# Low parts of the FFN's activations on GpSimd, bias of the output product on VectorE, in a schedule of its own

## What is computed

```
xn = layernorm(x)
q, k, v = xn @ wq + bq, xn @ wk + bk, xn @ wv + bv      # 16 heads of 16, rotary embedding on q and k
a  = softmax(causal(q k^T / 4)) v
s  = a @ wo + bo
h  = silu(xn @ w_gate^T) * (xn @ w_up^T)                # hidden width 768, int8-range weights / 127
g  = silu(h @ w_down^T)
out = x + s * g
```

## Time and profile before

| | us |
|---|---|
| median of 3 runs (lowest, highest) | 553.73 (550.44, 556.63) |
| profiled execution: whole time | 555.2 |
| profiled execution: span of the profile | 553.7 |
| TensorE busy in it | 480.0 (87%) |
| VectorE busy | 425.1 (77%) |
| GpSimd busy | 332.1 (60%) |
| ScalarE busy | 330.0 (60%) |

### The profile page before, as it was taken

One profiled execution on the slowest core, in us unless ns is written; L12 is line 12 of the kernel. 1 busy time (PEld: TensorE's weight loads), 2 busy tenths in 40 slices (PEclk: granted clock), 3 DMA queues, 4 the chain that ended last, 5 costly groups with the idle time before them and its releaser, 6 DMA issues.

```text
span 553.7 us, 13804 instructions
## 1 busy us (share of the span) xinstructions
PE 480.0 (87%) x5397; PEld 367.7 (66%) x5397; DVE 425.1 (77%) x667; ACT 330.0 (60%) x683; POOL 332.1 (60%) x439
## 2 busy tenths in 40 slices
PE   0679899979989999998999988999999988889873
PEld 0466797857667766785778675777668666558633
DVE  3398879946898799978996798769987768875713
ACT  2663256645785666666666756655674756663670
POOL 2114087745687938876779658598747646425452
PEclk9989799997999999999999999999989989977988
DMA  9356214394436856645753833578535575862021
GB/s 290 110 178 167 83 53 135 114 213 128 105 75 212 197 160 181 158 130 148 170 140 95 223 85 88 160 176 216 136 93 134 164 174 155 158 151 64 3 78 38
DMA packets 59667, 76.65 MB, mean 138 GB/s; under 512 B 15056, under 2 KB 30928, under 8 KB 59600
## 3 DMA queue, kind: packets, MB, share of 16 engines
q1 hardware_dynamic: 58512, 74.68, 51.4%
q10 hardware_dynamic: 1088, 1.05, 0.6%
HBM read 41.91 MB, written 29.82 MB: 130 GB/s over the span
## 4 chain that ended last, share of the span: by engine, by line
PE 38%; DVE 25%; DMA 13%; ACT 8%; issue 7%; SPq 6%; POOL 2%; DVEq 0%; ACTq 0%; POOLq 0%
PE ps_w L618 22%; DVE row_max L982 9%; PE ps_w L749 5%; DMA sum_rows<-o_t 5%; PE ps_w L647 4%; ACT probs L863 4%; PE ps_w L663 4%; DMA at_lo<-inv_rows 4%; DVE h_lo L434 3%; DVE hid L1028 2%; DVE hid L1023 2%; DVE attn L991 2%; PE ps_w L650 2%; DVE high_low L972 1%; SPq L549 1%
## 5 line engine op out<-in xcount | busy, mean ns | idle before, releaser
L982 DVE TENSOR_REDUCE row_max<-ps_w 128x2 f32<-128x1024 f32 (+3 forms) x256 | 199.7, 815 | 42.0 <-PE ps_w L650 41.6
L863 ACT ACTIVATE probs<-ps_w 128x512 f32<-128x512 f32 (+1 forms) x384 | 181.0, 535 | 78.1 <-PE ps_w L663 65.2
L1094 POOL TENSOR_SCALAR_AFFINE_SELECT probs<-probs 128x256 f32<-128x256 f32 x256 | 109.4, 449 | 123.1 <-ACT probs L863 122.9
L647 PE MATMUL ps_w<-k_st,q_st 48*128 48x512 f32 (+3 forms) x512 | 80.8, 355 | 19.5 <-DVE row_max L982 6.5
L663 PE MATMUL ps_w<-q_st,k_st 49*128 49x512 f32 (+3 forms) x512 | 78.8, 353 | 16.0 <-DMA q_st<-minus_max 5.8
L618 PE MATMUL ps_w<-xt_hi,wgu_hi 64*128 64x512 f32 x384 | 84.9, 430 | 3.0 <-DVE wgu_lo L961 1.3
L618 PE MATMUL ps_w<-xt_lo,wgu_hi 64*128 64x512 f32 x384 | 80.4, 407 | 0.0
L749 PE MATMUL ps_w<-probs,vals 128*32 128x512 f32 (+3 forms) x1024 | 79.1, 450 | 0.7 <-POOL probs L1094 0.4
L647 PEld LDWEIGHTS ps_w<-k_st,q_st 48*128 48x128 f32 x512 | 49.1, 195 | 39.8 <-issue 11.8
L663 PEld LDWEIGHTS ps_w<-q_st,k_st 49*128 49x128 f32 x512 | 47.2, 193 | 35.0 <-ACT probs L863 8.7
L749 PEld LDWEIGHTS ps_w<-probs,vals 128*32 128x32 f32 x1024 | 29.1, 112 | 41.0 <-issue 29.7
(11 more groups left out here) (106 smaller groups left out, 904.3 us busy)
## 6 DMA issues: line engine op xcount, KB each, us to landing
parts_q<-high_low SPq DMA_DIRECT2D x48, 256.0 KB, 3.2
q_st<-parts_q SPq DMA_DIRECT2D x64, 192.0 KB, 3.6
k_st<-parts_k SPq DMA_DIRECT2D x64, 192.0 KB, 4.7
parts_k<-high_low SPq DMA_DIRECT2D x42, 256.0 KB, 3.4
xn<-L_attn_x SPq DMA_DIRECT2D x8, 512.0 KB, 4.0
res<-L_attn_x SPq DMA_DIRECT2D x8, 512.0 KB, 6.2
result<-res SPq DMA_DIRECT2D x8, 512.0 KB, 3.6
attn<-o_t SPq DMA_DIRECT2D x112, 32.0 KB, 2.6
```

Of the source, the lines that this page charges most:

```text
L647: pe.matmul(dst[h][:, col:col + (t + 1) * P], q_st[64 * h:64 * h + STACK, pair, t * P:(t + 1) * P], k_st[64 * h:64 * h + STACK, pair, 0:(t ...
L863: nc.scalar.activation(probs[:, (pair % 2) * SLOTS + slot, col:col + WIDTH[c]], w_of(kind, b, 3 * pair + c // 2, c % 2)[:, 0:WIDTH[c]], AC ...
L982: last = nc.vector.tensor_reduce(of_pair, both_of(kind, b, i)[:, :, col:col + (t + 1) * P], AX.X, ALU.max)
L1094: nc.gpsimd.affine_select(out=v, in_=v, compare_op=ALU.is_ge, fill=0.0, base=0, pattern=[[0, 2], [1, P]], channel_multiplier=-1).then_inc( ...
```

## The change

`POOL_LOWS` becomes all six tiles, so that the subtraction of `low_part` runs on GpSimd for each of the 48 hidden tiles. The items `GB` (GpSimd) and `BO` (ScalarE) and their semaphores go. In `OP`, VectorE first adds `bo_row`, unscaled, to the product in PSUM, in place, and then does the multiplication it did. The rest of the program text is as it was, but the table of orders is another on all five engines.

```diff
-POOL_LOWS = ()
+POOL_LOWS = (0, 1, 2, 3, 4, 5)
...
     "pool": """
-        WC0.0 WQ0.0 RS0.0 RP3.0 RP4.0 RS0.1 NM0.1 NM1.1 NM2.1 NM3.1 RP0.1 RP1.1 RP3.1 RP4.1 RS0.2 B0.0 NM0.2 RP6.1 NM1.2 B1.0 NM2.2 NM3.2
+        WQ0.0 RS0.0 RP3.0 RP4.0 RS0.1 WC0.0 HL0.0 HL1.0 NM0.1 NM1.1 NM2.1 NM3.1 HL2.0 HL3.0 HL4.0 RP0.1 RP1.1 HL5.0 RP3.1 B0.0 RP4.1 RS0.2
...
         def add_x(eng, tensor_tensor, b, i):
             need(eng, prod_ready, 2 * b + i + 1)
-            need(eng, bias_added, 2 * b + i + 1)
+            if i == 0:
+                need(eng, res_in, 16 * (b + 1))
...
-                elif kind == "BO":
-                    act.wait_ge(bias_in, 16 * 4)
-                    nc.scalar.activation(bo_row[:], bo_row[:], ACT.Identity, scale=0.5 * WSCALE).then_inc(bo_scaled, 1)
...
                 elif kind == "OP":
                     wait_full(dve, "dve", kind, b, 0, i)
                     ps = w_of(kind, b, 0, i)
-                    need(dve, bias_added, 2 * b + i + 1)
+                    by_tile = lambda ap: ap.rearrange("p (a d) -> p a d", d=DM)
+                    if b == 0 and i == 0:
+                        dve.wait_ge(bias_in, 16 * 4)
+                    nc.vector.tensor_tensor(by_tile(ps[:, :]), by_tile(ps[:, :]), by_tile(bo_row[:]).broadcast_to([P, 2, DM]), ALU.add)\
+                        .then_inc(sum_ready, 1)
+                    need(dve, sum_ready, 2 * b + i + 1)
                     nc.vector.scalar_tensor_tensor(out=gate[:, b % 2, i, :], in0=ps[:, :], scalar=0.5 * WSCALE, in1=gate[:, b % 2, i, :],
                                                    op0=ALU.mult, op1=ALU.mult).then_inc(prod_ready, 1)
...
-                elif kind == "GB":
...
-                    need(pool, silu_ready, 2 * b + i + 1)
-                    need(pool, *rope_t_used[-1])
-                    need(pool, bias_added, 2 * b + i)
...
-                    nc.gpsimd.tensor_tensor(by_tile(rope_t[:]), by_tile(gate[:, b % 2, i, :]), by_tile(bo_row[:]).broadcast_to([P, 2, DM]), ALU.mult)\
-                        .then_inc(gate_biased, 1)
...
-                    nc.gpsimd.tensor_tensor(r, r, rope_t[:], ALU.add).then_inc(bias_added, 1)
```

More of the change, by code:

```diff
@@ new lines @@
+        B23.1@45 U1.3 A9.2@23 PV3.1@4 A10.2@01 B0.2@57 V0.3@23 A11.2@01 A12.2@45 B1.2@67 V1.3 MT1.2@01 B2.2@67 B3.2@45 G2.3@01 A13.2@67
+        B4.2@24 U2.3 G3.3@35 B5.2@24 A14.2@67 U3.3 B6.2@02 PV0.2@4 B7.2@03 A15.2@12 A16.2@67 B8.2@45 B9.2@03 G4.3@12 B10.2@45 A17.2@67
+        G5.3@03 U4.3 MT2.2@45 U5.3 B11.2@45 OP0.1@67 XT0.4@45 XT1.4@01 OP1.1 A18.2@23 B12.2@45 PV1.2@0 B13.2@16 A19.2@23 QK0.4@45 A20.2@67
+        A21.2@01 B14.2@23 QK1.4 A22.2@67 A23.2@23 DN0.3@01 MT3.2@23 A0.3@45 B15.2@67 B16.2@23 DN1.3 B17.2@23 A1.3@45 B18.2@67 PV2.2@2
@@ new lines @@
+        A6.7@45 B21.6@67 MT0.7@23 A7.7@01 B22.6@23 A8.7@45 A9.7@67 B23.6@01 PV3.6@2 A10.7@01 A11.7@67 B0.7@45 B1.7@23 B2.7@01 B3.7@45
+        A12.7@67 MT1.7@23 A13.7@01 A14.7@23 A15.7@67 A16.7@45 DN0.7@01 A17.7@23 A18.7@67 B4.7@45 DN1.7 MT2.7@23 B5.7@45 B6.7@67 PV0.7@2
+        A19.7@34 B7.7@01 A20.7@56 OP0.6@27 B8.7@01 A21.7@34 B9.7@56 OP1.6 ON0.7@01 B10.7@34 B11.7@56 B12.7@01 A22.7@34 A23.7@56 PV1.7@2
+        MT3.7@34 B13.7@01 ON1.7@23 B14.7@45 B15.7@67 B16.7@01 B17.7@23 B18.7@45 B19.7@67 PV2.7@0 B20.7@12 B21.7@34 B22.7@56 ON2.7@01
@@ L143 @@
+        B23.7@27 AT0.7@34 PV3.7@5 ON3.7@01 AT1.7@01 OP0.7@01 OP1.7
     """,
     "act": """
[L145 to L147 removed]
@@ L219 @@
+        B0.6 B1.6 B2.6 HL0.7 B3.6 B4.6 B5.6 B6.6 HL1.7 B7.6 B8.6 HL2.7 B9.6 B10.6 B11.6 AD0.5 AD1.5 HL3.7 B12.6 B13.6 B14.6 B15.6 B16.6
+        B17.6 B18.6 B19.6 B20.6 B21.6 B22.6 B23.6 HL4.7 B0.7 HL5.7 B1.7 B2.7 B3.7 B4.7 B5.7 B6.7 B7.7 B8.7 B9.7 B10.7 AD0.6 B11.7 B12.7
+        AD1.6 B13.7 B14.7 B15.7 B16.7 B17.7 B18.7 B19.7 B20.7 B21.7 B22.7 B23.7
     """,
@@ L1069, in do @@
                         rope_t_used.append(rope_at(b, i // 6, i % 6 + 2))
-                elif kind == "GB":
-                    if b == 0 and i == 0:
-                        pool.wait_ge(bo_scaled, 1)
-                    need(pool, silu_ready, 2 * b + i + 1)
-                    need(pool, *rope_t_used[-1])
-                    need(pool, bias_added, 2 * b + i)
-                    by_tile = lambda ap: ap.rearrange("p (a d) -> p a d", d=DM)
-                    nc.gpsimd.tensor_tensor(by_tile(rope_t[:]), by_tile(gate[:, b % 2, i, :]), by_tile(bo_row[:]).broadcast_to([P, 2, DM]), ALU.mult)\
-                        .then_inc(gate_biased, 1)
-                    need(pool, gate_biased, 2 * b + i + 1)
-                    if i == 0:
-                        need(pool, res_in, 16 * (b + 1))
-                    r = res[:, 2 * i:2 * i + 2, :].rearrange("p t d -> p (t d)")
-                    nc.gpsimd.tensor_tensor(r, r, rope_t[:], ALU.add).then_inc(bias_added, 1)
-                    rope_t_used.append((bias_added, 2 * b + i + 1))
                 elif kind == "HL":
```

232 lines of the change are left out of this document (109 added, 123 removed).

## The result

The changed kernel is faster by 4.7%, and the prediction (547.0, range 537 to 561) is wrong: the time lies outside the range, and the gain is four times the one forecast.

A forecast was written before the change was run, and what follows sets the result against it. TensorE was taken as nearest to a bound, its idle time being what can be won. From 555.2 us, -12.6 (VectorE), +0.6 (GpSimd), +4 (later low parts), +1.3 (end) and -1.5 (median) gave 547.0 us, range 537 to 561.

The forecast's parts named there:

- The new order at nothing: All engines' lists: reordering the same work can't be costed from rows; put at 0, range widened some 5 us each side.
- VectorE's relief, 37% of 34.0, -12.6: VectorE: 44.9 us of low parts leave, 10.9 of additions come; 37%, `h_lo`'s chain share of its busy time, reaches the end.
- GpSimd's balance, +0.6: GpSimd: 43.6 us of bias work out, 62.4 of low parts in; 18.8 more, mostly covered by idle time, costing +0.6 us.
- the wait for `res`: GpSimd's 7.7 us wait for `res` in the old trace disappears; counted as nothing because GpSimd was idle anyway.
- The low part later, +4: ScalarE's tanh waits longer for slower low parts on GpSimd: 10 us at 12 places, 40% counted, +4 us; bounds 0 and 30.
- The end, +1.3: After TensorE's last product, two bias additions stand in the open on VectorE, each 0.68 + 0.03 us: +1.3 us, bounds 1.2 and 1.9.
- The price of an addition: Bias additions on VectorE with one operand in PSUM: 0.68 us each, 10.9 us for 16, no contention with GpSimd's reads.
- VectorE busy at 385 to 397: Sign of the forecast: VectorE's busy time at 390 us, between 385 and 397, with `high_low` still near 0.95.
- the port rival: VectorE and GpSimd delay each other reading SBUF, so moving work returns what it saves: 552 us, to 556; chance 0.05.
- Slower: GpSimd stands at low parts with masks behind, holding up `PV`: some 18 us added, 565 us, range 558 to 570; chance 0.18.
- More than forecast: All VectorE's relief arrives because TensorE's idle time is short waits hanging on the maxima: 535 us; chance 0.08.

The follow-up runs named there:

- the load test: Changed kernel with 48 more VectorE reductions that nobody reads, 676 ns each, against the changed kernel: 537.53 us, ratio 0.9673, 1.4 points above it.
- the mixed kernels: Old or new lists with work divided otherwise, moved items placed by input readiness; against before, new lists with old division 551.17 us, old lists with new division 565.48.
- the run with SyncE's list alone: SyncE's list taken from the new order, against the kernel with old lists and new division (565.48 us): 610.5 us, ratio 1.1016.

## Why the prediction was wrong, step by step

- **The new order at nothing.** This is the step that failed: "the same work in another order can't be costed from rows ... I put 0 and widen the range by some 5 us to each side". With the old work the order is worth 3.8 us, inside the 5 to each side. But it doesn't stand beside the other terms as one more summand. Without it the division costs 10.5 us, with it the division brings 22. The two rows of the sum that I took as independent, order and division, have a joint term of 33 us, larger than all the others.
- **The same miss, counted in the new lists.** There the parts add up, and the prediction's terms can be set beside them one by one. Low parts: forecast -16.6 + 2.1 + 4 = -10.5 us, measured 2.2 points, -12. Bias: forecast 4.0 - 1.4 + 1.3 = +3.9, measured 1.9 points, -10.6. Order alone: 0, measured -3.8. Counted so, most of the 20 us by which the forecast is off lies in the bias. But in the kernel that gives its 1.9 points the bias work was placed by rule, so they are not the price in a list made for it, and the near agreement of the low parts is in part luck: its +4 was near 0.
- **VectorE's relief, 37% of 34.0, -12.6.** In the new lists a measured load counts at 24%, which makes 34.0 us worth 8; with its interval of 6 to 42% it can't refute the 37. Even the 37% explains less than half of the gain. In the old lists 26.5 us less busy time on VectorE (425.1 to 398.6), together with more work on GpSimd, brought no gain at all. So the share of the chain was no safe estimate of what removal gives back, the doubt that the prediction's last sentence named.
- **GpSimd's balance, +0.6, and the wait for `res` "behind which GpSimd was idle anyway".** Mis-sized. Taking the bias off GpSimd and onto VectorE is worth 1.9 points (10.6 us) in the new lists; with it on GpSimd `OP` waits for it 15.4 us and `PV` for masks 10.1. How much of this a better place for it would save wasn't tested. GpSimd's idle time is no spare time where others wait for what stands in its queue.
- **The low part later, +4.** The tanh instructions waited for low parts 3.3 us, where I had 10, so in these lists the term is near 0. It is not small by nature: a single low part misplaced by four instructions in the first batch costs 4 to 6 us, while 17 in later batches cost nothing that shows.
- **The end, +1.3.** Right. Four operations of VectorE stand there (start, us, engine, line):

```profile
516.80 0.70 DVE L1015 TENSOR_TENSOR ps_w<-ps_w,bo_row 128x512 f32<-128x512 f32 x1 [3.59 <-PE ps_w L617]
517.54 0.69 DVE L1018 SCALAR_TENSOR_TENSOR gate<-ps_w,gate 128x512 f32<-128x512 f32 x1
518.15 0.69 DVE L1015 TENSOR_TENSOR ps_w<-ps_w,bo_row 128x512 f32<-128x512 f32 x1
518.87 0.69 DVE L1018 SCALAR_TENSOR_TENSOR gate<-ps_w,gate 128x512 f32<-128x512 f32 x1
519.48 1.28 DVE L439 TENSOR_TENSOR res<-res,gate 128x512 f32<-128x512 f32 x2
```

  From the first of them to `res` it is 2.68 us, before 1.20: 1.5 more.
- **The price of an addition.** 691 ns, where I took 680. The Trainium skill (SBUF — State Buffer, "Who interferes with whom") has it that an operand in PSUM keeps an instruction out of GpSimd's way. The trace agrees: 691 ns on average and 700 at most, while `high_low`, with both inputs in SBUF, rose from 946 to 1031 on average.
- **VectorE busy at 385 to 397.** It is 403.0. The groups by line lost 44.9 and gained 11.1 for the additions, but `high_low` (+2.8 us) and the sum into `attn` (+1.8) take longer than before. And the groups of before add up to 451.0 where the page has 425.1 busy, because neighbours overlap by some hundredths of a us (518.15 starts before 517.54 + 0.69). So taking a group out lowers the busy time by less than the group's sum. The stretch that the port rival foresaw is there, some 5 us in these two groups, and small; that `high_low` would stay near 0.95 us was wrong.
- **TensorE's busy time.** The sum had no term for it, and it gave 12.0 of 29.4 us. The mean granted clock rose from 0.95 to 0.972, and the mean of the score products for the maxima fell from 355 ns (`L647`) to 346 (`L646`). Busy time times mean clock is 456.0 before and 454.9 now, so the clock accounts for nearly all of the 12.0.
- **The rivals.** "Slower" is what the division does in the old lists, at the place it named. There 23 low parts have a mask right behind them, and in the new lists also 23, where the masks aren't late: which neighbours an instruction has in a list says little without the times at which all of them are ready. *More than forecast* puts 25 us into its sum for "all of VectorE's relief". With the 34.0 of its own balance it would be 525.6, close to the 527.07 measured. That would have been luck: by the load test VectorE's relief is worth 2 to 14 us.

What stays open: which of the lists of TensorE, VectorE and ScalarE carries the joint term, and how much of it is the placing by rule in the mixed kernels. Kernels with one of these three lists taken over alone weren't run. TensorE's new list is more than another order: 485 of its 570 items with a PSUM bank have another bank than before, so the choice of banks is part of what is called order here.

## What to carry to other kernels

Where every engine's order is written out, work and order are one change: moving instructions between engines by a balance of busy time, each put where its input was ready, gave +1.9%, and the same move with lists made for it -4.0%, so price a move only with its lists, and try it only with them. An instruction's cost in such a list is what waits behind it and for it, and the filling of the pipeline is the place to look first: in the new lists one instruction of 1.3 us put behind four others there cost 4 to 6 us of the whole, and 17 such moves in later batches cost nothing that shows. A load test asks directly what an engine's time is worth, where a share of the chain only suggests it; but at 24%, between 6 and 42, it needs a larger load or more runs to decide.

## What the runs showed of the hardware

TensorE's busy time follows its granted clock. All 20 kernels run the same 5397 products, and busy time times mean clock is between 451.3 and 456.7 us in every one, from the changed kernel (468.0 us, 0.972) to the run with SyncE's list alone (493.8 us, 0.921). The slower kernels, with more idle time of TensorE, mostly have the lower clock: idle for 56.3 us at 0.972, for 73.7 at 0.950 (before), for 115.0 at 0.921. The relation is loose, since 58.4 us of idle time stand beside 0.954 in the run with one low part moved.

Where the clock falls shows in rows of 20 us. The number after 20.00 is TensorE's busy time, and the one after the five engines its granted clock. Before:

```profile
60.00:80.00 20.00, 18.78 (x211) 16.90 (x213) 15.69 (x29) 8.71 (x18) 9.35 (x9) 0.83 0.24 68
480.00:500.00 20.00, 16.71 (x150) 10.02 (x148) 14.41 (x22) 10.89 (x26) 5.78 (x14) 0.78 0.61 146
```

Changed:

```profile
60.00:80.00 20.00, 19.68 (x240) 17.75 (x240) 11.65 (x23) 7.68 (x16) 14.03 (x15) 0.91 0.58 136
460.00:480.00 20.00, 18.70 (x179) 14.11 (x181) 13.52 (x21) 8.35 (x20) 7.07 (x14) 0.74 0.51 122
```

A mean between 0.5 and 1 is a stretch with parts at 1.2 GHz and parts at 2.4. At 60 to 80 us the changed kernel has 0.9 us less idle and 0.91 for 0.83; over 50 to 500 us 0.98 for 0.96. Near the end the lowest such row is 0.78 before and 0.74 in the changed kernel. That the closed gaps caused the higher clock was not tested by itself.

The stretch of instructions with both inputs in SBUF, on VectorE beside GpSimd, is uneven: before, the low parts took 676 to 1774 ns; in the changed kernel the 16 additions, with one input in PSUM, took 685 to 700.
